# A fused attention and feed-forward kernel: the second stage's work order in tables of half steps

## The chip, the cores and the metric

The kernel runs on one core of one Trainium2 chip. The metric is device time in microseconds, from the launch to the end on that core.

## The reference

For x of 4 batches x 1024 rows x 512 columns (f32) the program computes, with xn the normalised rows:

```
xn = layernorm(x)
q, k, v = xn Wq^T, xn Wk^T, xn Wv^T          # 16 heads of 32, 4 batches: 64 (batch, head) pairs
p = softmax(causal(q k^T / sqrt(32)))         # 1024 x 1024 for each head
a = (p v) Wo^T
g = silu((xn Gate) * gate_scale);  u = (xn Up) * up_scale      # 512 -> 1536, weights rounded to fp8 values
f = ((g * u) Down) * down_scale               # 1536 -> 512
out = x + a + f
```

## The kernel before, in words

The first stage (`prepare`, about the first 285 us) normalises x, forms q, k and v and writes them to DRAM. The second stage (`attend`) is the one that is changed. It loops over 16 iterations (`NIT`), and each iteration over 4 heads (`s` = 0 to 3), so head n = 4 it + s of 64. A head's work is cut into steps `u`, and k counts the steps of the whole iteration. Every engine has its own program, written by walking the same steps and asking tables what is to be done at each; the engines then meet through semaphores. Nothing reorders the work afterwards: each engine, and the SP queue that issues the DMAs, takes its instructions strictly in the written order.

Numbers are kept as two fp16 parts, high and low, hence many operations come in pairs. The names used below:

- PE: `scores` of unit 0 to 5 (called E0 to E5 here; L1457), `scores_of_row` for the last two blocks of rows (R0, R1; L1471, L1475), `maxima_scores` of unit 0 to 7 for head n+2 (M0 to M7; L210), `values` of row block i for head n-1 (PV0 to PV7; L1495), `turn_maxima` (TURN; L263), gate and up products of feed-forward part f (G0 to G11 and U0 to U11; L1519), `down` of half i and piece j (DN(i,j); L1533), and `project` (PJ; L1541). Down works on the tile of the iteration before; project runs only from iteration 4 on (`LAG`).
- ACT: the exponential of unit u (exp0 to exp5, L1273), its high part (L1263), the exponential of a row block (L1280) and its high part (L1287), `tanh_of_gate` (L1294), `high_of_fuse` (L1302), `high_maxima` (L247, written as m_part), and the high part of the attention rows (L1330).
- DVE: maxima (L233, L238, L1399), low parts, `swiglu`, `normalise`, `copy_row` (L270), `scale_down` and `add_output` (L1371).
- POOL: causal selection, low parts (L1064, L1216, L1198, L1194), `low_maxima`.

What ties them where the change touches them: R1 overwrites a pair of banks that unit 2's exponential must have read; M0 overwrites the bank of the first row block, so it waits for that block's exponential; G0 needs the tile of xn that SP loads (`load_tile`, L1088), and SP may only issue this load when U11 of the last tile has been done; PV7 needs the second row block of the head before, turned by a DMA (`turn_row`, L1100) that SP issues behind that load. TURN's result is copied by DVE into a row, which SP stores into the next head's q (`store_row`, L200); E0 of the next head waits for it. DN(1,0) needs the copy made of the TURN before it, since both use the bank `misc`. `start_values` makes PE wait for the low parts of all units.

```
pe.wait_ge(exp_done, NE * n + 3)                     # R1
pe.wait_ge(row_exp, 2 * n + 1)                       # M0
pe.wait_ge(xt_loaded, 16 * (it + 1))                 # G0
pe.wait_ge(row_turned[ROWS.index(i)], 16 * (n + 1))  # PV6, PV7
```

Of the kernel before, what the change touches and what calls it, by code (L numbers as in the profile page):

```python
# [47 lines left out]
HEADS_PER_IT = 4  # L48
# [58 lines left out]
U = 9  # L107
# [29 lines left out]
DOWN_STEP = {0: [(0, 0), (0, 1)], 1: [(0, 2)], 2: [(0, 3)], 3: [(0, 4)], 4: [(0, 5)],
             9: [(1, 0), (1, 1)], 10: [(1, 2)], 11: [(1, 3)], 12: [(1, 4)], 13: [(1, 5)]}  # L140
# [24 lines left out]
def of_head(table, n, u):


    found = [(table[u], n)] if u in table else []
    if u + U in table and n > 0:
        found.append((table[u + U], n - 1))  # L170
    return found
# [884 lines left out]

# [642 lines left out]
```

## Time and profile before

| | |
|---|---|
| median of 3 timed runs | 1288.54 us |
| lowest, highest | 1285.94, 1290.28 us |
| span of the profiled execution | 1287.4 us |
| first matmul of the second stage | 287.67 us |
| PE busy | 1230.8 us, 96% |
| DVE, ACT, POOL busy | 80%, 70%, 68% |

No time of its own is listed for the profiled execution beside its span, which runs from the first instruction to the last. Matmuls overlap one another in the array, so the duration of one (276 ns for 256 columns) is longer than the distance to the next; the distances between starts tell how fast PE goes.

### The profile page before, as it was taken

What the parts mean: (1) busy time and instruction counts of PE and PEld (TensorE: products, weight loads), DVE (VectorE), ACT (ScalarE), POOL (GpSimd) and SP (SyncE); (2) the same over time, 40 slices, a digit from 0 to 9 for tenths busy, and PEclk for the clock granted to TensorE, in tenths of its full rate; (3) what the DMA queues carried; (4) which work ended last, traced back from release to release, by engine and by line L of the source; (5) the groups of instructions that cost most, each with busy time, mean ns of one, the idle gap of its engine ahead of it and who ended that gap; (6) DMA issues with size and microseconds to landing.
All of it is one profiled execution on the core that took longest, in us unless ns stands there. A gap on an engine that the chain in (4) does not pass through costs nothing.

```text
span 1287.4 us, 32439 instructions
## 1 busy us (share of the span) xinstructions
PE 1230.8 (96%) x11756; PEld 822.8 (64%) x11756; DVE 1036.1 (80%) x2615; ACT 895.2 (70%) x1527; POOL 873.5 (68%) x1017
## 2 busy tenths in 40 slices
PE   4999999997999999999999999999999999999988
PEld 3444444445766767676777677777767677777663
DVE  8888887877877888788878788888888888878762
ACT  4322323228878888788888788888878888888770
POOL 1333232107877787788888888978878788888882
PEclk9999999998999999999999999999999999999999
DMA  8599998855645475666667676767686766767655
GB/s 271 161 250 243 256 258 232 203 152 120 135 96 129 96 151 99 145 114 148 127 138 153 127 153 125 157 104 166 115 158 114 160 121 137 143 128 165 105 113 121
DMA packets 427599, 196.07 MB, mean 152 GB/s; under 512 B 339248, under 2 KB 396592, under 8 KB 427440
## 3 DMA queue, kind: packets, MB, share of 16 engines
q1 hardware_dynamic: 409024, 177.22, 63.2%
q10 hardware_dynamic: 18416, 16.78, 4.9%
q8 instruction: 94, 1.54, 0.5%
q14 instruction: 65, 0.53, 0.1%
HBM read 72.89 MB, written 42.21 MB: 89 GB/s over the span
## 4 chain that ended last, share of the span: by engine, by line
PE 40%; POOL 16%; ACT 8%; issue 6%; DVE 5%; DMA 2%; SPq 0%; ACTq 0%; POOLq 0%; DVEq 0%
PE bank L1519 12%; PE bank L1533 12%; POOL row L1216 7%; PE bank L1495 6%; PE pair L210 3%; PE pair L1457 3%; POOL fuse L1198 3%; POOL probs L1064 3%; ACT probs L1263 3%; PE pair L1471 2%; POOL p L1210 2%; DMA p_t<-row 2%; ACT row L1287 2%; PE pair L1541 2%; DVE row_top L1399 2%
## 5 line engine op out<-in xcount | busy, mean ns | idle before, releaser
L1273 ACT ACTIVATE p<-pair,s_exp 128x512 f32<-128x512 f32 (+1 forms) x384 | 243.4, 634 | 143.3 <-PE pair L1457 142.0
L1216 POOL TENSOR_TENSOR row<-row 128x896 f16<-128x896 f32 (+1 forms) x128 | 256.2, 2011 | 7.7 <-ACT row L1287 7.7
L1263 ACT CAST probs<-p 128x512 f16<-128x512 f32 (+1 forms) x384 | 214.9, 560 | 15.1 <-POOL p L1210 12.6
L1064 POOL TENSOR_TENSOR probs<-p,probs 128x512 f16<-128x512 f32 x192 | 221.1, 1155 | 0.2
L1519 PE MATMUL bank<-shared,wu 128*128 128x256 f16 x1536 | 202.7, 276 | 0.0
L1519 PE MATMUL bank<-shared,wg 128*128 128x256 f16 x1536 | 202.5, 275 | 0.0
L1533 PE MATMUL bank<-wd,fuse 128*128 128x512 f16 x768 | 191.7, 380 | 0.8 <-DVE ff_out L1380 0.8
L1399 DVE TENSOR_REDUCE row_top<-pair 128x1 f32<-128x896 f32 (+1 forms) x128 | 147.5, 1152 | 35.4 <-PE pair L1475 34.9
L1210 POOL TENSOR_SCALAR_AFFINE_SELECT p<-p 128x128 f32<-128x128 f32 (+1 forms) x256 | 109.6, 433 | 93.2 <-ACT p L1273 91.3
L1198 POOL TENSOR_TENSOR fuse<-fu,fuse 128x512 f16<-128x512 f32 x96 | 118.5, 1235 | 65.3 <-ACT fuse L1302 65.1
L1519 PEld LDWEIGHTS bank<-shared,wg 128*128 128x128 f16 x1536 | 143.2, 98 | 25.0 <-DMA shared<-xn_parts 0.8
L1519 PEld LDWEIGHTS bank<-shared,wu 128*128 128x128 f16 x1536 | 144.1, 99 | 22.3 <-issue 0.2
L1280 ACT ACTIVATE row<-pair,row_bias,s_exp 128x896 f32<-128x896 f32 (+1 forms) x128 | 148.3, 1158 | 0.3 <-DVE row_bias L1402 0.3
L233 DVE CUSTOM_DVE_ANT_0 junk<-pair,mask 128x128 bf16<-128x128 f32 x252 | 116.8, 482 | 34.9 <-PE pair L210 34.2
L1457 PE MATMUL pair<-q_st,k_st 98*128 98x256 f16 (+3 forms) x640 | 136.5, 278 | 1.2 <-PEq L285 1.0
L1495 PE MATMUL bank<-v_sb,probs 128*128 128x65 f16 x2688 | 134.3, 193 | 2.6 <-DVE attn L1362 2.6
L1495 PEld LDWEIGHTS bank<-v_sb,probs 128*128 128x128 f16 x2688 | 120.0, 97 | 25.2 <-issue 3.0
L210 PE MATMUL pair<-k_st,q_st 96*128 96x128 f16 x504 | 125.5, 309 | 7.6 <-issue 6.9
L1287 ACT CAST row<-row 128x896 f16<-128x896 f32 (+1 forms) x128 | 126.7, 990 | 0.0
L1387 DVE SCALAR_TENSOR_TENSOR ga<-th,bank 128x256 f32<-128x256 f32 x192 | 79.7, 415 | 43.8 <-ACT th L1294 43.6
L1064 DVE TENSOR_TENSOR probs<-p,probs 128x512 f16<-128x512 f32 (+1 forms) x192 | 112.1, 597 | 2.1 <-ACT probs L1263 2.1
L1533 PEld LDWEIGHTS bank<-wd,fuse 128*128 128x128 f16 x768 | 68.6, 97 | 61.1 <-issue 1.4
(155 smaller groups left out, 2106.0 us busy)
## 6 DMA issues: line engine op xcount, KB each, us to landing
q_st<-q_parts SPq DMA_DIRECT2D x192, 64.0 KB, 2.3
k_st<-k_parts SPq DMA_DIRECT2D x192, 64.0 KB, 2.0
v_parts<-res SPq DMA_DIRECT2D x8, 1056.0 KB, 6.8
v_sb<-v_parts SPq DMA_DIRECT2D x64, 132.0 KB, 2.2
xn_parts<-x_t SPq DMA_DIRECT2D x16, 512.0 KB, 8.8
q_parts<-qk_st SPq DMA_DIRECT2D x32, 256.0 KB, 5.5
k_parts<-qk_st SPq DMA_DIRECT2D x32, 256.0 KB, 4.2
shared<-xn_parts SPq DMA_DIRECT2D x16, 512.0 KB, 4.9
```

The costliest lines, as they stand in the source:

```text
L210: nc.tensor.matmul(banks[u % len(banks)][:, 0:w], rows.q_st[i][part, blk * P:(blk + 1) * P], rows.k_st[i][part, k0:k0 + w], start=True, st ...
L1064: ops.tensor_tensor(probs[n % 2][:, LO, at], p32[e % RING][:, 0:UNIT_WIDTH[u]], probs[n % 2][:, HI, at], ALU.subtract).then_inc(signal, 1)
L1198: nc.gpsimd.tensor_tensor(fuse_pair(LO, p), fu[p % FU][:, :], fuse_pair(HI, p), ALU.subtract).then_inc(fuse_lo, 1)
L1216: nc.gpsimd.tensor_tensor(row16[r][:, w:2 * w], row32[r][:, :], row16[r][:, 0:w], ALU.subtract).then_inc(row_lo, 1)
L1263: nc.scalar.copy(probs[n % 2][:, HI, u * 512:u * 512 + w], p32[e % RING][:, 0:w]).then_inc(p_hi, 1)
L1273: nc.scalar.activation(p32[e % RING][:, 0:w], st_bank[u % 2][:, 0:w], ACT.Exp, scale=s_exp[:, :]).then_inc(exp_done, 1)
L1287: nc.scalar.copy(row16[r][:, 0:row_width(r)], row32[r][:, :]).then_inc(row_hi, 1)
L1399: nc.vector.tensor_reduce(row_top[:, r:r + 1], row_bank[r][:, 0:row_width(r)], AX.X, ALU.max).then_inc(row_red, 1)
L1457: mm = nc.tensor.matmul(st_bank[u % 2][:, at:at + w], k_st[s][:, j * P:(j + 1) * P], q_st[s][:, q0:q0 + w], start=True, stop=True)
L1495: mm = nc.tensor.matmul(o_half[:, i % (QB // 2), :], probabilities(n, i, j, part), v_sb[s][:, j, 0:VN], start=(j == 0 and part == HI), sto ...
L1519: mm = nc.tensor.matmul(ff_bank[f % 2][:, h * FT:(h + 1) * FT], (wg8, wu8)[h][:, kc, f * P:(f + 1) * P], xt[:, part, kc, :], start=(part = ...
L1533: mm = nc.tensor.matmul(misc[:, :], fuse[:, part, f, i * P:(i + 1) * P], wd8[:, f, :], start=(f == 0 and part == HI), stop=(f == FC - 1 an ...
```

## The change

The tables get 18 half steps per head where there were 9 steps, one table for each kind of operation and engine, and PE's feed-forward tables exist twice: for iterations 0 to 3 (EARLY) and for 4 to 15 (LATE). Most entries are the old ones doubled. What stands elsewhere than before (half steps of a head, or of the iteration where the table runs over four heads):

- PE: M3 from 12 to 11 (ahead of E3); PV1 from 2 to 3 (behind the down or project piece of step 2); the wait for all low parts from PV7 to PV5; DN(1,0) from the start of head 1 to the end of head 0; TURN of head 2 behind U7; in late iterations G0 from 8 to 7, G1 from 12 to 9, G10 from 62 to 61; in early iterations U0 from 10 to 8, U9 from 54 to 57, G11 from 66 to 65.
- ACT: `high_maxima` from behind exp1 and the high part of unit 0 to ahead of exp1; the high part of the attention rows one half step earlier in head 1; `high_of_fuse` of pair 0 from 30 to 28 in early iterations.
- DVE: the reduction of M5 from 14 to 13, which puts it ahead of `swiglu` 0 in head 0.
- POOL: the low part of the attention rows from 42 to 40 in head 2, and in late iterations that of fuse pair 4 from 60 to 63, behind the first row block.

```diff
-U = 9
+U = 18
...
-M_STEP = {4: (0, 1), 5: (2,), 6: (3, 4), 7: (5,), 8: (6, 7)}
-PV_STEP = {1: (0, 1), 2: (2,), 3: (3,), 5: (7,), 6: (6,), 7: (5,), 8: (4,)}
+M_STEP = {8: (0, 1), 10: (2,), 11: (3,), 12: (4,), 14: (5,), 16: (6, 7)}
+PV_STEP = {2: (0,), 3: (1,), 4: (2,), 6: (3,), 10: (7,), 12: (6,), 14: (5,), 16: (4,)}
+UNITS_FOR = {0: 3, 5: NE}
...
+def of_ffn(what, it, k):
+    found = []
+    for i, at in ((it - 1, k + STEPS), (it, k)):
+        if 0 <= i < NIT:
+            found += [(f, i) for f in (LATE_FF if i >= LAG else EARLY_FF)[what].get(at, ())]
     return found
...
                         if n > 0:
-                            if u in (1, 5):
-                                start_values(n - 1, (s + 3) % 4, it if s == 0 else it + 1, 3 if u == 1 else NE)
                             for i in PV_STEP.get(u, ()):
+                                if i == 0:
+                                    pe.wait_ge(v_loaded[(s + 3) % 4], 16 * (it if s == 0 else it + 1))
+                                if i in UNITS_FOR:
+                                    start_values(n - 1, UNITS_FOR[i])
                                 values(n - 1, (s + 3) % 4, i)
```

PE in head 3 of iteration 1 (an early one), before: the third row is G9, the fourth U9, then come E1 (two rows), R0 (three), PV0 and PV1 (x6), E2.

```order
L1519 MATMUL bank<-shared,wu 128x256 x8
L1457 MATMUL pair<-q_st,k_st 128x512
L1519 MATMUL bank<-shared,wg 128x256 x8
L1519 MATMUL bank<-shared,wu 128x256 x8
L1457 MATMUL pair<-q_st,k_st 128x384
L1457 MATMUL pair<-q_st,k_st 128x128
L1471 MATMUL pair<-k_st,q_st 128x512
L1471 MATMUL pair<-k_st,q_st 128x384
L1475 MATMUL pair<-mask_bf,ident_bf 128x128
L1495 MATMUL bank<-v_sb,probs 128x65 x6
L1457 MATMUL pair<-q_st,k_st 128x256 x2
```

The same place in the changed kernel:

```order
L1527 MATMUL bank<-shared,wu 128x256 x8
L1467 MATMUL pair<-q_st,k_st 128x512
L1527 MATMUL bank<-shared,wg 128x256 x8
L1467 MATMUL pair<-q_st,k_st 128x384
L1467 MATMUL pair<-q_st,k_st 128x128
L1481 MATMUL pair<-k_st,q_st 128x512
L1481 MATMUL pair<-k_st,q_st 128x384
L1485 MATMUL pair<-mask_bf,ident_bf 128x128
L1505 MATMUL bank<-v_sb,probs 128x65 x6
L1527 MATMUL bank<-shared,wu 128x256 x8
L1467 MATMUL pair<-q_st,k_st 128x256 x2
```

U9 moved from ahead of E1 to ahead of E2; what stands ahead of E2 is the same in all.

PE in head 0 of a late iteration, from PV3 (x8) on, before: DN(0,4), M0, M1, DN(0,5), G0, M2, PV7 (x16), U0, and at the end TURN and G1.

```order
L1495 MATMUL bank<-v_sb,probs 128x65 x8
L1533 MATMUL bank<-wd,fuse 128x512 x4
L210 MATMUL pair<-k_st,q_st 128x128
L210 MATMUL pair<-k_st,q_st 128x256
L1533 MATMUL bank<-wd,fuse 128x512 x4
L1519 MATMUL bank<-shared,wg 128x256 x8
L210 MATMUL pair<-k_st,q_st 128x384
L1495 MATMUL bank<-v_sb,p_t 128x65 x16
...
L1495 MATMUL bank<-v_sb,p_t 128x65 x14
L263 MATMUL bank<-ident,m_part 12x128
L1519 MATMUL bank<-shared,wg 128x256 x8
```

The same place in the changed kernel:

```order
L1505 MATMUL bank<-v_sb,probs 128x65 x8
L1541 MATMUL bank<-wd,fuse 128x512 x4
L1527 MATMUL bank<-shared,wg 128x256 x8
L225 MATMUL pair<-k_st,q_st 128x128
L225 MATMUL pair<-k_st,q_st 128x256
L1541 MATMUL bank<-wd,fuse 128x512 x4
L1527 MATMUL bank<-shared,wg 128x256 x8
L225 MATMUL pair<-k_st,q_st 128x384
L1505 MATMUL bank<-v_sb,p_t 128x65 x16
...
L1505 MATMUL bank<-v_sb,p_t 128x65 x14
L278 MATMUL bank<-ident,m_part 12x128
```

G0 now stands ahead of M0, and G1, which stood behind TURN, ahead of M2 and PV7.

ACT in head 3 of iteration 1, before: tanh and `high_of_fuse` of part 8 and pair 3, exp1, the high part of unit 0, `high_maxima`, tanh and exp2.

```order
L1294 ACTIVATE th<-bank,half_gs 128x256
L1302 CAST fuse<-fu 128x512
L1273 ACTIVATE p_3<-pair,s_exp 128x512
L1263 CAST probs<-p_2 128x512
L247 ACTIVATE m_part<-mx 128x6
L1294 ACTIVATE th<-bank,half_gs 128x256
L1273 ACTIVATE p_4<-pair,s_exp 128x512
```

The same place in the changed kernel:

```order
L1314 ACTIVATE th<-bank,half_gs 128x256
L1322 CAST fuse<-fu 128x512
L262 ACTIVATE m_part<-mx 128x6
L1293 ACTIVATE p_3<-pair,s_exp 128x512
L1283 CAST probs<-p_2 128x512
L1314 ACTIVATE th<-bank,half_gs 128x256
L1293 ACTIVATE p_4<-pair,s_exp 128x512
```

Only the small m_part row moved, from behind exp1 and a high part to ahead of exp1.

## Rows read from the trace of the kernel before

**Rows 1.** The page: busy time of the engines; clock granted to PE in 40 slices.

```profile
PE 1230.8 (96%) x11756; PEld 822.8 (64%) x11756; DVE 1036.1 (80%) x2615; ACT 895.2 (70%) x1527; POOL 873.5 (68%) x1017
...
PEclk9999999998999999999999999999999999999999
```

**Rows 2.** Busy times of a stretch: PE, PEld, DVE, ACT, POOL, clock, DMA share, GB/s.

```profile
600.00:700.00 100.00, 99.86 (x1084) 72.81 (x1081) 84.30 (x238) 84.96 (x151) 82.59 (x92) 1.00 0.65 133
```

**Rows 3.** PE's waits, whole span: us in total, times, longest.

```profile
PE pair L1471 <- ACT p L1273: 13.7, 11, 1.6
...
PE pair L210 <- issue: 6.9, 10, 0.9
...
PE bank L1495 <- DMA p_t<-row: 2.6, 3, 1.0
```

**Rows 4.** Timeline of PE, iteration 1, head 3 (start, us, engine, line, operation).

```profile
392.28 1.04 PE L1519 MATMUL bank<-shared,wu 128*128 128x256 f16 x8
393.15 0.38 PE L1457 MATMUL pair<-q_st,k_st 98*128 98x384 f16 x2
...
393.99 0.38 PE L1457 MATMUL pair<-q_st,k_st 98*128 98x256 f16 x2
...
395.87 0.60 PE L1471 MATMUL pair<-k_st,q_st 96*128 96x512 f16 x2 [1.31 <-ACT p L1273]
```

**Rows 5.** Timeline of ACT in the same head.

```profile
392.74 0.62 ACT L1302 CAST fuse<-fu 128x512 f16<-128x512 f32 x1
393.57 0.69 ACT L1273 ACTIVATE p<-pair,s_exp 128x512 f32<-128x512 f32 x1 [0.21 <-PE pair L1457]
...
394.67 0.21 ACT L247 ACTIVATE m_part<-mx 128x6 f16<-128x6 f32 x1
...
395.13 0.69 ACT L1273 ACTIVATE p<-pair,s_exp 128x512 f32<-128x512 f32 x1
```

**Rows 6.** Busy times of two stretches around such waits (columns as in rows 2).

```profile
379.00:385.00 6.00, 5.02 (x46) 3.62 (x47) 4.34 (x14) 5.21 (x8) 4.50 (x7) 0.72 0.33 86
440.00:446.00 6.00, 3.96 (x51) 3.13 (x51) 5.66 (x17) 6.00 (x11) 4.24 (x8) 1.00 0.53 123
```

**Rows 7.** Timeline of PE, head 0 of iterations 10 and 6: M0 and PV7.

```profile
951.17 0.33 PE L210 MATMUL pair<-k_st,q_st 96*128 96x128 f16 x2
...
954.44 0.34 PE L1495 MATMUL bank<-v_sb,p_t 128*128 128x65 f16 x6 [1.03 <-DMA p_t<-row]
...
711.46 0.33 PE L210 MATMUL pair<-k_st,q_st 96*128 96x128 f16 x2
...
714.52 0.47 PE L1495 MATMUL bank<-v_sb,p_t 128*128 128x65 f16 x10 [0.75 <-DMA p_t<-row]
```

**Rows 8.** Timeline of SP at those two places: issues of the load and the turning.

```profile
945.78 0.57 SPq L1088 DMA_DIRECT2D shared<-xn_parts  x1
946.45 3.71 SPq L1100 DMA_TRANSPOSE p_t<-row  x1
...
705.91 0.73 SPq L1088 DMA_DIRECT2D shared<-xn_parts  x1
```

**Rows 9.** From issue to landing: load 945.78, turning 946.45, load 705.91.

```profile
DMA to landing us min/median/max: 4.5/4.5/4.5
...
DMA to landing us min/median/max: 7.9/7.9/7.9
...
DMA to landing us min/median/max: 6.6/6.6/6.6
```

**Rows 10.** Timeline of PE (TURN, head 2; E0, head 3) and SP, iteration 8.

```profile
807.34 0.22 PE L263 MATMUL bank<-ident,m_part 128*12 128x128 f16 x1
...
808.64 0.65 SPq L200 DMA_DIRECT2D q_st<-m_row  x1
...
811.46 0.38 PE L1457 MATMUL pair<-q_st,k_st 98*128 98x512 f16 x1
```

**Rows 11.** DMA throughput from 808.6 to 812.0 us in 40 slices.

```profile
GB/s 0 0 0 0 0 0 0 0 0 0 0 0 0 0 0 15 21 0 0 0 0 0 0 51 166 220 217 226 208 214 220 205 208 202 184 214 157 238 389 401
```

More of the change, by code:

```diff
@@ L162, in at_step @@
+def of_ffn(what, it, k):
[3 more added lines that the diff above has]
+            found += [(f, i) for f in (LATE_FF if i >= LAG else EARLY_FF)[what].get(at, ())]
     return found
 def of_head(table, n, u):
[L168 to L171, printed above, removed]
+    found = [(what, n - 1) for what in table.get(u + U, ())] if n > 0 else []
+    return found + ([(what, n) for what in table.get(u, ())] if n < NH else [])
@@ L1055, in over_iterations, with over_steps @@
                 step(it, it >= LAG)
+        def over_steps(step):
+            for it in range(NIT):
+                for s in range(HEADS_PER_IT):
+                    for u in range(U):
+                        step(it, s, u)
+            for u in range(U):
+                step(NIT, 0, u)
         def take_low(eng, ops, units, u, n, signal):
@@ L1332, in _, with step @@
-            over_iterations(iteration)
-            take_high(NE - 1, NH - 1)
-            for k in range(STEPS, STEPS + 3):
-                for f, t in at_step(TANH_STEP, NIT - 1, k):
+            def step(it, s, u):
+                n, k = HEADS_PER_IT * it + s, s * U + u
+                for unit, head in of_head(EXP_STEP, n, u):
+                    exponentials(unit, head)
+                for unit, head in of_head(HIGH_STEP, n, u):
+                    take_high(unit, head)
+                for r, head in of_head(ROW_EXP_STEP, n, u):
+                    exponentials_of_row(r, head)
+                for r, head in of_head(ROW_HIGH_STEP, n, u):
+                    high_of_row(r, head)
+                for _, head in of_head(MAX_HIGH_STEP, n, u):
+                    if head + 1 < NH:
+                        high_maxima(nc, act, rows, head + 1, (head + 1) % 2)
+                for f, t in of_ffn("tanh", it, k):
@@ L1336, in _ @@
                     tanh_of_gate(f, t)
-                for p, t in at_step(FUSE_STEP, NIT - 1, k):
+                for p, t in of_ffn("fuse_high", it, k):
                     high_of_fuse(p, t)
+                if LAG <= it < NIT:
+                    for i in SPLIT_STEP.get(k, ()):
+                        r = it - LAG
+                        act.wait_ge(o_done, 2 * HEADS_PER_IT * it)
+                        wait(act, turned, 16 * (2 * r + i))
+                        nc.scalar.copy(a_part[:, HI, :], attention_rows(i, r)).then_inc(split_link, 1)
@@ L1608, in _ @@
                 down(0, piece, NIT - 1)
[L1609 to L1610 removed]
+            for i in (7, 6):
+                values(NH - 1, 3, i)
+            start_values(NH - 1, NE)
+            for i in (5, 4):
                 values(NH - 1, 3, i)
```

212 lines of the change are left out of this document (97 added, 115 removed).

## The prediction

> **What bounds the kernel now.** I read the page's busy times first: PE 96%, DVE 80%, ACT 70%, POOL 68% [rows 1]. Busy PE could hide gaps, since matmuls overlap, so I then cut the span into stretches. From 600 to 700 us PE is busy for 99.86 of 100 us, with the full clock, while DVE, ACT and POOL stand at 83 to 85% [rows 2]. In the timeline the starts are packed too: eight matmuls of 256 columns take 0.87 us from the first to the next group (392.28 to 393.15, rows 4), that is 109 ns each, and 256 columns at 2.4 GHz are 107 ns. So from iteration 4 on (about 540 us) the kernel is a solid block of PE work, the same work in both kernels, and reordering it can win only what PE waits there. PE's waits, summed over the whole span, name all that matters [rows 3]: 13.7 us in 11 waits of R1 (L1471) for ACT's exponential of unit 2, 6.9 us in 10 waits of M0 (L210) for the first row block's exponential, and 2.6 us in 3 waits of PV7 for the turned rows. The first two lie almost wholly in iterations 0 to 3, where heads 2 and 3 (in iteration 0 all heads) have no down and no project pieces between E2, R1 and M0. The third lies in late iterations. All of it is some 23 us, under 2% of the span, and the change touches a part of it. A difference within 0.3% (3.9 us) can't be told from none here; the three runs lie 4.3 us apart.
>
> **U9 behind R0, and high_maxima ahead of exp1 (early head 3, four times).** In head 3 of iteration 1, PE issues U9 at 392.28, E1 at 393.15, E2 at 393.99, and R1 only at 395.87, after a wait of 1.31 us [rows 4]. ACT ends the fuse cast at 393.26 (the next could start there: 392.74 + 0.62 less the 0.1 by which records overlap), but exp1 starts at 393.57, having been idle 0.21 us for E1. Then follow a high part, m_part at 394.67, tanh, and exp2 at 395.13 [rows 5]. From exp1 to exp2 are 1.56 us of ACT without a gap, of which m_part is 0.10 (394.67 to the next start at 394.77). Now E1 comes 0.87 us earlier, so ACT no longer waits for it: exp1 gains its 0.31 us (393.57 less 393.26), gives 0.10 to m_part which now stands ahead of it, and gets the 0.10 back before exp2. So exp2, R1, the row block's exponential and M0 come 0.31 us sooner. The tanh between needs U9, which now ends some 0.3 us before ACT comes to it; E2 has the same work ahead of it and keeps its place. Four heads: 4 x 0.31 = **1.2 us gained**. The bounds: nothing, if U9's delay makes tanh late by as much, and 4 x (0.31 + 0.10) = 1.6.
>
> **high_maxima elsewhere.** In early head 2 and in the heads of iteration 0, ACT has a queue ahead of exp1 already, so m_part only moves ahead of it and exp2 starts as before: 0, at most 6 x 0.10 = 0.6. In late heads R1 waits for nothing: 0.
>
> **G0 and G1 ahead of M0 and PV7 (late head 0, twelve times).** Between M0 and PV7 stood M0, M1, DN(0,5), G0, M2: 2.07 us where nothing waits. Now G0 and G1 come ahead as well, and PV7 stands 2 x 0.87 - 0.87 = 0.87 us later in the order. That gives the turned rows 0.87 us more. But G0 now stands where M0 stood, 1.04 us earlier, so the load of xn has that much less. In iteration 10 M0 is at 951.17 and PV7 at 954.44, 1.20 us late [rows 7]. The load landed at 945.78 + 4.5 = 950.28, before G0's new place; the turning landed at 946.45 + 7.9 = 954.35 [rows 8, 9], and PV7's new place is 951.17 + 2.07 + 0.87 = 954.11. So a wait of 1.20 becomes 0.3: 0.9 gained. In iteration 6 PV7 was 0.99 us late (714.52 less 711.46 and 2.07); there the load landed at 705.91 + 6.6 = 712.51 [rows 7 to 9], and G0's new place is 711.46, so G0 now waits 1.05 and PV7 no longer. That is 0.1 lost: the wait changes its name and not its size. Since both transfers sit in one queue, one behind the other, this exchange is the rule. Of the twelve, four are late at all; by the same sums the other two give a loss of 0.1 and nothing. I take **0.7 us gained**. Bounds: all of PV7's waits, 2.6 us [rows 3], gained, and, if every load landed a microsecond later than G0's new place with the turning close behind, 12 x 0.1 = 1.2 lost.
>
> **What costs nothing, and its cover.** DN(1,0) at the end of head 0 needs the copy of TURN. From TURN to the next head's E0 are 4.12 us (807.34 to 811.46), and store_row, which needs the copy, is issued 1.30 us after TURN [rows 10]. DN(1,0) now stands two feed-forward groups nearer, at 4.12 - 2 x 0.87 = 2.4 us, so 1.1 us are spare. It also makes head 1's exp0 0.87 us later, but ACT had over a microsecond of idle time ahead of exp1 there. TURN in head 2 moves behind U7, so the row has 3.25 us instead of 4.12 to reach the next E0. The store is issued at 808.64, and its few packets run in the 16th and 17th slice of 0.085 us, 1.4 us later [rows 10, 11]. TURN at 808.21 plus 0.6 for the copy, 0.2 for SP and 1.4 gives 810.4, against 811.46: a microsecond spare. M3 ahead of E3 needs only M1 reduced, G10 ahead of M0 leaves M0 there before DVE, which is still normalising, comes to it. PV1 and the wait for the low parts moved behind work that was ready. On POOL the attention part and the fuse pair change places with parts of which the rows to be turned profit by about 0.7 us, but SP is then still busy with issues ahead of the turning, so it stays there. DVE's M5 ahead of swiglu 0 delays G2's release by 0.7 us, and G2 stands more than that behind.
>
> On the row's landing a rule bears: the Trainium skill, in DMA: Bandwidth & Descriptors (Anatomy of one DMA), gives a transfer a fixed cost of about 2.0 us, most of it the receipt after the last byte. By it the row would be there at about 808.21 + 0.8 + 2.0 = 811.0 (an estimate from that page), still ahead of E0, so the sum would be the same but with 0.4 us spare, not 1.1. The trace shows no landing for this store, only its packets.
>
> **Sum.** 1.2 + 0.7 = 1.9 us. The profiled execution's span goes from 1287.4 to about 1285.5; the median of the runs is 1.1 above that span, so 1288.5 - 1.9 = **1286.6**.
>
> **The rivals.**
> *The clock goes with the waits.* The stretch 379 to 385 had a mean granted clock of 0.72, though 440 to 446, with the same kind of waits, had 1.00 [rows 6]. PE fell to 1.2 GHz for 0.28 x 6 / 0.5 = 3.4 us, which loses 1.7 us of work at 2.4 GHz. I count five such dips after waits of R1 and M0 in iterations 0 to 3, two of them in head 3. If shorter waits there keep the clock up, 2 x 1.7 = 3.4 us come on top, and five would be 8.5: 1283.2, at the extreme 1278. Against it: the wait only shrinks from 1.31 to 1.0, and equal waits end both ways. Chance 0.2.
> On this the Trainium skill, in TensorE: Matmul & The Clock Gate (Part 1), says that the gate's phase is free-running and the cold part varies from run to run. By that such dips would come and go without the change; the trace, with waits alike and dips unlike, agrees.
> *The order is covered everywhere, nothing moves.* If U9's tanh takes back what E1 gives and PV7's wait only becomes G0's, the time is 1288.5. It is on the near side of my forecast, and the measurement couldn't tell them. Chance 0.25.
> *Head 3's E0 waits for the row (slower).* If the store's receipt comes 3.25 us after TURN or later, PE waits at E0 in all 16 iterations; it decides from there on. With a landing 0.3 us past it the cost is 16 x 0.3 = 4.8 less 1.9: 1291.4. For it speaks that this is the only place where cover was taken away for all iterations at once, against it the 1.1 us above. Chance 0.1, together with the like at DN(1,0).
> The forecast as worked out has 0.45.
>
> **How the numbers follow.** Forecast and "nothing moves" both lie within 0.3% (1284.7 to 1292.4). Some of the clock rival lies faster than 1284.7, as does a small part of the forecast (several small gains of the kind that no single wait shows). The slower rival passes +3.9 us only when large. So faster 0.27, same 0.66, slower 0.07. The range runs from 1283.2, the clock rival's time, to 1289.8, which takes in "nothing moves" with the runs' own spread of over a microsecond, and leaves out the slower rival and the extreme of the clock.
>
> **What would show it.** In the changed kernel's timeline R1's wait in head 3 of iterations 0 to 3 is near 1.0 us and in head 2 still 1.4; U9 stands between R0 and E2. In late head 0 waits for the load of xn appear at G0 (L1527) where those for turned rows at PV7 shrink. PE from 600 to 700 stays at 99.8 or 99.9 us. No wait appears at E0 of head 3 or DN(1,0). The prediction is wrong if a new wait repeats in every iteration, if more or fewer dips of the clock come in iterations 0 to 3, or if iterations 4 to 15, at some 60 us each, get shorter by more than PV7's waits.

## The result and the profile after

The changed kernel takes **1277.61 us** (median of 6 runs, 1276.75 to 1279.67) against 1289.41 us (1285.94 to 1292.1, 6 runs) for the kernel before beside it: a ratio of 0.9914, 95% interval 0.99 to 0.9927, or 11.1 us less by the ratio and 11.8 by the medians. Forecast were 1286.6 us, range 1283.2 to 1289.8. The gain is far larger than the forecast's and the time lies below the range. Two runs at a much lower clock are set aside in all medians, ratios and clocks: one of act_group (2096.08 us, clock 0.569) and one of the kernel before (1311.86 us, 0.944).

The profile page of the changed kernel (busy times; clock granted to PE in 40 slices; shares of the chain that ended last), as in [rows 1]:

```profile
PE 1229.0 (96%) x11756; PEld 820.5 (64%) x11756; DVE 1048.7 (82%) x2615; ACT 891.3 (70%) x1527; POOL 871.0 (68%) x1017
...
PEclk9999999998999999999999999999999999999999
...
PE 65%; ACT 3%; POOL 3%; issue 2%; DMA 2%; DVE 1%; SPq 0%; ACTq 0%; POOLq 0%
```

Busy times look as before. The last row doesn't: the same row of the kernel before, which I had not drawn on, is

```profile
PE 40%; POOL 16%; ACT 8%; issue 6%; DVE 5%; DMA 2%; SPq 0%; ACTq 0%; POOLq 0%; DVEq 0%
```

POOL, ACT and DVE, 29% of what had set the end, are down to 7%. The stretch 600 to 700 us (columns as in [rows 2]) is now wholly PE:

```profile
600.00:700.00 100.00, 100.00 (x1115) 73.88 (x1113) 85.76 (x239) 85.94 (x152) 85.60 (x92) 1.00 0.63 135
```

PE's waits, whole span, as in [rows 3] (R1 is now L1481, M0 L225, values L1505, G0 L1527):

```profile
PE pair L1481 <- ACT p L1293: 10.3, 10, 1.4
PE pair L225 <- issue: 6.3, 10, 0.8
...
PE bank L1527 <- DMA shared<-xn_parts: 0.8, 1, 0.8
...
PE bank L1505 <- DMA p_t<-row: 0.3, 1, 0.3
```

R1's waits fall by 3.4 us, M0's by 0.6, those for turned rows by 2.3, and 0.8 come back at G0. Summed, this is 5.5 us, half of what was gained, and even that is too much: a wait that shrinks can come back elsewhere in pieces too short to be marked.

The timeline gives the rest. I measure an iteration from TURN in head 3 to TURN in the next head 3, and split the span at the TURNs of head 15 (head 3 of iteration 3) and 59 (head 3 of iteration 14). TURN prepares the next head, so the last head, 63, has none, and eleven late iterations end in a TURN of head 3:

| stretch of the profiled execution, us | before | after |
|---|---|---|
| start to first E0 | 287.67 | 286.14 |
| E0 to TURN of head 15 | 233.87 | 229.95 |
| TURN of head 15 to TURN of head 59, 11 late iterations | 659.22 | 655.13 |
| of these, one without a wait for DMA | 59.68 | 59.43 |
| rest | 106.60 | 105.69 |

**Late iterations** are each 0.25 us shorter where PE waits for no DMA: 11 x 0.25 = 2.75; the other 1.3 are the waits for the load and for turned rows. These vary from one execution to the next: the stretch takes 659.22 us here and 658.80 to 660.40 in four other executions with the same late order, while the changed kernel has 655.13 and 655.10 (the table under the experiments). Where does a solid block of PE work get 0.25 us? Before, head 3 of the iteration whose E0 is in [rows 10] ends so (timeline of PE):

```profile
820.17 0.66 PE L1495 MATMUL bank<-v_sb,p_t 128*128 128x65 f16 x16
820.95 0.22 PE L263 MATMUL bank<-ident,m_part 128*12 128x128 f16 x1
821.11 0.39 PE L1457 MATMUL pair<-q_st,k_st 98*128 98x256 f16 x2
```

and after, in one of the late iterations:

```profile
753.51 0.65 PE L1505 MATMUL bank<-v_sb,p_t 128*128 128x65 f16 x16
754.09 0.22 PE L278 MATMUL bank<-ident,m_part 128*12 128x128 f16 x1
754.24 0.39 PE L225 MATMUL pair<-k_st,q_st 96*128 96x512 f16 x1
```

From PV7's start to TURN's are 0.78 us before and 0.58 after, and it is so in all eleven (0.78 to 0.80, and 0.58 or 0.59). TURN waited 0.2 us; only 0.13 to 0.15 of it are idle time of PE, too short to be marked as a wait. The other 0.05 lie ahead of PV7 in the same head. What released it stands in the chain of the kernel before, 804 to 821 us (start, us, what; 15 of its pieces, from POOL's fuse on):

```profile
804.92 1.16 POOL fuse L1198
806.08 1.11 POOL a_part L1194
807.19 1.12 POOL probs L1064
808.31 3.93 POOL row L1216 x2
812.25 0.71 POOL p L1210
...
813.03 0.04 ACT probs L1263
...
813.24 0.48 ACT th L1294
...
813.74 0.43 DVE ga L1387
...
814.20 0.48 DVE fu L1394
814.68 1.01 DVE row_top L1399
...
817.57 1.15 DVE row_top L1399
...
819.39 0.07 DVE attn L1362
...
820.23 0.67 DVE shared L1371
820.91 0.04 issue
820.95 0.22 PE bank L263
```

Read upwards from the last row: TURN waits for `add_output` (both use `misc`), which stands behind M0's and M1's maxima, `normalise` and `row_top` on DVE; DVE was late from ACT's tanh, tanh from the high part ahead of it, and that from POOL's causal selection, which stood behind 3.93 us of rows and, before them, the low part of the attention rows (`a_part`). The two ends of the link on ACT, before and after:

```profile
813.03 0.30 ACT L1263 CAST probs<-p 128x128 f16<-128x128 f32 x1 [0.47 <-POOL p L1210]
```

```profile
745.89 0.29 ACT L1283 CAST probs<-p 128x128 f16<-128x128 f32 x1
```

**Early iterations.** In head 3, R1 waited 1.31 us [rows 4], and now:

```profile
388.37 0.38 PE L1467 MATMUL pair<-q_st,k_st 98*128 98x512 f16 x1
...
390.59 1.03 PE L1527 MATMUL bank<-shared,wu 128*128 128x256 f16 x8
391.46 0.38 PE L1467 MATMUL pair<-q_st,k_st 98*128 98x256 f16 x2
...
392.77 0.60 PE L1481 MATMUL pair<-k_st,q_st 96*128 96x512 f16 x2 [0.74 <-ACT p L1293]
```

Head 2 goes from 1.40 to 1.21. Yet an early iteration with the full clock takes 59.05 us before and 58.71 after, 0.34 less and not the 0.76 by which the two waits shrink. In head 3 R1 starts 4.40 us after E0, for 4.69 before, and not 0.57 sooner, because PV0 now starts 0.29 us later behind R0 (0.35 us after R0's last piece, for 0.06). Behind the two feed-forward parts that follow M0 and M1, M2 then comes 0.13 us later than before, and 0.06 in head 2.

**The clock.** Such an iteration with one stretch at 1.2 GHz takes 60.7 us before and 60.2 after. From E0 to TURN 15, before has five stretches at 1.2 GHz, after has three (one of double length). Over its six runs the changed kernel has a mean granted clock of 0.9947. The clocks of the six runs of the kernel before beside it are not listed; five other sets of it have means of 0.9912 to 0.9919. A run at half the clock for part of its time loses (1 - mean clock) x time: 10.4 to 11.3 us before and 6.8 after, so 3.6 to 4.5 us of the 11.

So the gain is 2.75 (late iterations) + 1.3 (waits for the load and turned rows, one execution each) + 1.4 (early, 4 x 0.34, with iteration 0 taken to be like the others) + 3.6 to 4.5 (clock), 9 to 10 us of the 11 to 12. The remaining 1 to 3 us stay open. The table's first stretch is no part of them: its order is the same in both kernels, and 1.4 of its 1.5 us are a wait of the first stage for a DMA (`x_t<-x_part`, 2.5 us before, 1.1 after). Nor are the 0.9 of its last stretch safe: a second execution of the changed kernel takes 104.58 us there, 1.1 less than this one.

### The profile page after: what moved, and what is told of

It is laid out like the page before. It is cut to its first block, busy times and chain, and to the rows that moved or that the text cites. A ratio compares the mean times of both kernels' runs of the same rounds, so it can differ in the third digit from the quotient of the medians.

```text
span 1276.9 us, 32439 instructions
## 1 busy us (share of the span) xinstructions
PE 1229.0 (96%) x11756; PEld 820.5 (64%) x11756; DVE 1048.7 (82%) x2615; ACT 891.3 (70%) x1527; POOL 871.0 (68%) x1017
## 4 chain that ended last, share of the span: by engine, by line
PE 65%; ACT 3%; POOL 3%; issue 2%; DMA 2%; DVE 1%; SPq 0%; ACTq 0%; POOLq 0%
PE bank L1527 22%; PE bank L1541 12%; PE bank L1505 10%; PE pair L225 6%; PE pair L1467 5%; PE bank L1549 4%; PE pair L1481 4%; PE pair L1549 2%; POOL row L1241 1%; ACT p L1293 1%; ACT probs L1283 1%; DMA a_t<-a_part 1%; PE bank L278 1%; DMA p_t<-row 1%; POOL probs L1089 1%
## 5 line engine op out<-in xcount | busy, mean ns | idle before, releaser
L1527 PE MATMUL bank<-shared,wg 128*128 128x256 f16 x1536 | 201.0, 274 | 1.3 <-DMA shared<-xn_parts 0.8
L1527 PE MATMUL bank<-shared,wu 128*128 128x256 f16 x1536 | 201.2, 274 | 0.0
L1541 PE MATMUL bank<-wd,fuse 128*128 128x512 f16 x768 | 194.6, 381 | 0.8 <-DVE ff_out L1393 0.8
L1527 PEld LDWEIGHTS bank<-shared,wg 128*128 128x128 f16 x1536 | 144.9, 98 | 34.4 <-DMA shared<-xn_parts 1.3
L1527 PEld LDWEIGHTS bank<-shared,wu 128*128 128x128 f16 x1536 | 143.0, 98 | 20.3
L1505 PEld LDWEIGHTS bank<-v_sb,probs 128*128 128x128 f16 x2688 | 127.0, 97 | 38.6 <-issue 3.8
L1505 PE MATMUL bank<-v_sb,probs 128*128 128x65 f16 x2688 | 142.9, 193 | 2.6 <-DVE attn L1375 2.2
L225 PE MATMUL pair<-k_st,q_st 96*128 96x128 f16 x504 | 134.8, 309 | 6.4 <-issue 6.3
L1089 DVE TENSOR_TENSOR probs<-p,probs 128x512 f16<-128x512 f32 (+1 forms) x192 | 125.7, 668 | 2.0 <-ACT probs L1283 2.0
L1223 POOL TENSOR_TENSOR fuse<-fu,fuse 128x512 f16<-128x512 f32 x96 | 111.9, 1166 | 18.8 <-ACT fuse L1322 17.7
L253 DVE TENSOR_REDUCE mx<-pair 128x1 f32<-128x512 f32 x128 | 88.0, 688 | 23.1 <-PE pair L225 21.3
```

What stands on the lines that cost most here:

```text
L225: nc.tensor.matmul(banks[u % len(banks)][:, 0:w], rows.q_st[i][part, blk * P:(blk + 1) * P], rows.k_st[i][part, k0:k0 + w], start=True, st ...
L1089: ops.tensor_tensor(probs[n % 2][:, LO, at], p32[e % RING][:, 0:UNIT_WIDTH[u]], probs[n % 2][:, HI, at], ALU.subtract).then_inc(signal, 1)
L1505: mm = nc.tensor.matmul(o_half[:, i % (QB // 2), :], probabilities(n, i, j, part), v_sb[s][:, j, 0:VN], start=(j == 0 and part == HI), sto ...
L1527: mm = nc.tensor.matmul(ff_bank[f % 2][:, h * FT:(h + 1) * FT], (wg8, wu8)[h][:, kc, f * P:(f + 1) * P], xt[:, part, kc, :], start=(part = ...
L1541: mm = nc.tensor.matmul(misc[:, :], fuse[:, part, f, i * P:(i + 1) * P], wd8[:, f, :], start=(f == 0 and part == HI), stop=(f == FC - 1 an ...
```

## The experiments

All kernels are the changed one with some tables put back: "old" means that all entries stand where they stood before. In each fence - is the kernel that the edit starts from. Ratios are to the kernel before on the same chip. The columns R1 are the waits in early heads 2 and 3; late is an iteration without a wait for DMA; 15 to 59 is the stretch of the table above; clock is the mean granted clock of the runs.

| kernel | median us | ratio, 95% interval | R1 | late | 15 to 59 | clock |
|---|---|---|---|---|---|---|
| neutral | 1288.92 | 1.0004, 0.9995 to 1.0013 | 1.39, 1.31 | 59.69 | 660.40 | 0.9918 |
| pool_split | 1285.42 | 0.9974, 0.9958 to 0.999 | 1.39, 1.31 | 59.43 | 657.45 | 0.9917 |
| after_split42 | 1282.86 | 0.9956, 0.9943 to 0.9969 | 1.21, 0.74 | 59.79 | 657.65 | 0.9935 |
| act_group | 1284.58 | 0.997, 0.9957 to 0.9983 | 1.21, 1.22 | 59.68 | 659.31 | 0.9926 |
| max_high | 1286.82 | 0.9991, 0.998 to 1.0002 | 1.39, 1.21 | 59.68 | 658.75 | 0.9926 |
| fuse28 | 1285.62 | 0.9981, 0.9969 to 0.9993 | 1.31, 1.31 | 59.69 | 659.40 | 0.9933 |
| pe_early | 1284.61 | 0.9967, 0.9955 to 0.9979 | 1.39, 0.74 | 59.69 | 658.80 | 0.994 |
| u9_only | 1285.96 | 0.9982, 0.9973 to 0.999 | 1.40, 0.74 | 59.69 | 659.75 | 0.9932 |
| pe_late | 1290.12 | 1.0015, 1.0003 to 1.0027 | 1.58, 1.31 | 59.79 | 659.09 | 0.9908 |
| no_pe_late | 1280.92 | 0.9937, 0.9925 to 0.9949 | 1.21, 0.74 | 59.42 | 656.41 | 0.9936 |
| no_pe_late2 | 1280.48 | 0.9934, 0.992 to 0.9947 | 1.21, 0.74 | 59.42 | 655.70 | 0.9936 |
| after_again | 1278.67 | 0.9924, 0.9909 to 0.9939 | 1.21, 0.74 | 59.43 | 655.10 | 0.9937 |
| pool_pe_late | 1288.62 | 1.0001, 0.9991 to 1.0011 | 1.58, 1.31 | 59.43 | 657.53 | 0.9913 |
| gates_late | 1297.64 | 1.007, 1.0055 to 1.0084 | 1.40, 1.31 | 60.56 | 668.50 | 0.9922 |
| gates_m5 | 1287.71 | 0.9996, 0.9985 to 1.0007 | 1.40, 1.31 | 59.67 | 657.82 | 0.9915 |
| pe_rest | 1291.97 | 1.0026, 1.0013 to 1.0039 | 1.58, 1.31 | 59.78 | 660.80 | 0.99 |
| fill_m0 | 1275.12 | 0.9897, 0.9882 to 0.9912 | 0.74, 0.74 | 59.43 | 654.79 | 0.997 |
| fill_r1 | 1296.16 | 1.0041, 1.0019 to 1.0063 | 0.36, 0.36 | 59.42 | 656.12 | 0.9901 |

**neutral: the new tables with every entry at its old place.** The diff is the sum of all the edits below taken back, and of one that no run tests alone: POOL's low part of fuse pair 4 in late iterations (60 to 63). It is in the changed kernel, after_split42 and the two no_pe_late, and not in pool_split; late iterations without a wait for DMA take 59.42 to 59.43 us with it (no_pe_late) and 59.43 without (pool_split), so it shows nothing there.

> The new tables filled with the old places, so every engine's order is that of the kernel before up to the last head. A control: 1.000, and heads' distances as before. If the form of the tables or the placing of the program had a share in the gain of 11 us, this would be faster.

Nothing is gained or lost. So the form of the program, its length and its loops are worth nothing, and the moves are all.

**pool_split: only POOL's low part of the attention rows (old otherwise).**

```diff
-SPLIT_LOW_STEP = {26: (0,), 42: (1,)}
+SPLIT_LOW_STEP = {26: (0,), 40: (1,)}
```

> The kernel before in half steps, with one move alone: POOL's low part of the attention rows in head 2 from half step 42 to 40. Theory A (POOL frees ACT): in late head 2 POOL no longer idles for a fuse pair, ends the two row blocks some 0.7 us sooner, ACT's wait for POOL's selection in head 3 goes (0.47 us before), and the tanh, swiglu, normalise and add_output that follow each other there come 0.3 us sooner, so TURN of head 3 no longer waits 0.3 us: 11 or 12 iterations x 0.25 to 0.3 = 2.7 to 3.4 us, about 1286.2. Theory B (PE's order did it, G10 ahead of M0): nothing here, 1289.4, and TURN still stands 0.3 us behind PV7.

**after_split42: the changed kernel with that one entry taken back.**

```diff
-SPLIT_LOW_STEP = {26: (0,), 40: (1,)}
+SPLIT_LOW_STEP = {26: (0,), 42: (1,)}
```

> The changed kernel with POOL's attention low part put back to half step 42. Theory A (POOL sets ACT, DVE and so TURN back): a late iteration without a DMA wait takes 59.7 to 59.8 us again for 59.43, 11 to 12 iterations: 3 to 4.5 us slower than the changed kernel, about 1281.5. Rival (in the full set PE's order alone holds TURN free): 1277.6.

The pair settles the late iterations. One entry on an engine that is 68% busy takes them from 59.69 to 59.43 us with the old order, and from 59.43 back to 59.79 with the new one, where TURN starts 0.83 us after PV7 and its wait is long enough to be marked:

```profile
755.01 0.22 PE L278 MATMUL bank<-ident,m_part 128*12 128x128 f16 x1 [0.18 <-DVE shared L1384]
```

11 x 0.26 = 2.9 of the 3.3 us that pool_split gained by its ratio (1.3 to 5.4 by the interval); in the stretch it is 660.40 - 657.45 = 2.95 against neutral, and less against the other executions of the old late order, which vary by 1.6. Taken back, the entry costs 4.2 to 5.3 us by the medians of the two measurements of the changed kernel. Of this, 657.65 - 655.13 = 2.5 are in the stretch (11 x 0.36 = 4.0, less 1.4, since the longer iterations leave no load late), and 0.3 to 1.5 are clock ((0.9937 or 0.9947 - 0.9935) x 1280). The last microsecond or so is not accounted for. Where the time lay on POOL, before and after:

```profile
804.92 1.16 POOL L1198 TENSOR_TENSOR fuse<-fu,fuse 128x512 f16<-128x512 f32 x1 [1.61 <-ACT fuse L1302]
```

```profile
736.54 1.16 POOL L1219 TENSOR_TENSOR a_part<-attn,a_part 128x512 f16<-128x512 f32 x1 [0.82 <-ACT a_part L1349]
```

Before, POOL stood idle for the fuse cast and had `a_part` still to do behind it; now it does `a_part` in that gap, and the rows follow 0.7 us sooner: they start 3.87 us ahead of head 3's E0 after (741.01 and 744.88) and 3.19 ahead of it before (808.27 and 811.46). ACT's high part behind the selection comes 0.56 us sooner by the same measure. The 0.7 us are those that the prediction gave the rows.

**act_group, max_high, fuse28: ACT's moves together, and two of them alone (old otherwise).**

```diff
-MAX_HIGH_STEP = {2: (0,)}
+MAX_HIGH_STEP = {1: (0,)}
-SPLIT_STEP = {24: (0,), 40: (1,)}
+SPLIT_STEP = {23: (0,), 40: (1,)}
-FUSE_HIGH_EARLY = {36: (1,), 42: (2,), 54: (3,), 60: (4,), 74: (5,), 30: (0,)}
+FUSE_HIGH_EARLY = {28: (0,), 36: (1,), 42: (2,), 54: (3,), 60: (4,), 74: (5,)}
```

> The kernel before in half steps, with ACT's moves alone: high_maxima ahead of exp1, the attention high part one half step earlier, high_of_fuse of pair 0 at 28 in early iterations. Theory A: R1's wait in head 2 of iterations 1 to 3 falls from 1.40 to about 1.21 us, because POOL gets its fuse pair and so its selection done sooner; 0.1 to 0.2 us in ten heads: 1 to 1.5 us, about 1288.2. Rival: m_part only changes places with exp1 and nothing moves, 1289.4, R1 still waits 1.40. Dips of the clock after these waits may add or take 1.7 us each.

> The kernel before in half steps, with high_maxima ahead of exp1 alone. Of the ACT group's 3.5 us the theory gives most to the fuse cast at 28 (POOL's fuse pair and selection sooner), so here: R1's wait in head 2 stays 1.40, in head 3 falls by 0.10 (1.31 to about 1.21), 4 x 0.1 us, 1288.5. Rival: high_maxima carries the group's gain, about 1285.5.

> Theory A: of the ACT group's gain only fuse pair 0 at half step 28 shortens R1's wait in early head 2, from 1.39 to about 1.2 us, through ACT and POOL's fuse pair; head 3 stays at 1.3 and late iterations at 59.7. Four heads of 0.19 are 0.8 us: 1288.0, a ratio of 0.9985 to 1. Rival: the cast only changes places with a tanh or an exponential, R1 keeps 1.39 in head 2, and the time is that of before (ratio 0.999 to 1.0015).

max_high has only the first pair, fuse28 only the third. `high_maxima` shortens R1's wait in head 3 by 0.10, and the iteration with the full clock not at all (59.07 us against 59.06 in neutral). The fuse cast takes 0.09 off R1's wait in head 2, and head 2 from TURN to TURN goes from 15.18 to 15.07; the remaining 0.1 in act_group (1.21) needs both. So neither expectation for fuse28 holds exactly: its 0.19 is the two moves' together. All three times fall by more than these tenths allow, and the clock is 0.9926 (act_group and max_high) and 0.9933 (fuse28) against 0.9918 (neutral).

**pe_early and u9_only: PE's early feed-forward pieces (old otherwise).**

```diff
-GATE_EARLY = {..., 62: (10,), 66: (11,)}
+GATE_EARLY = {..., 62: (10,), 65: (11,)}
-UP_EARLY = {10: (0,), 14: (1,), ..., 52: (8,), 54: (9,), 62: (10,), 68: (11,)}
+UP_EARLY = {8: (0,), 14: (1,), ..., 52: (8,), 57: (9,), 62: (10,), 68: (11,)}
```

> The kernel before in half steps, with PE's early tables alone (U9 behind R0, G11 and U0 earlier, iterations 0 to 3). By the prediction's step: R1 in head 3 comes 0.2 to 0.3 us sooner four times, about 1 us: 1288.4. Theory that the clock goes with these waits: two or three dips of 1.7 us vanish on top, 1284 to 1286. Rival: G11 ahead of E3 takes it back, 1289.4.

> The kernel before in half steps, with U9 behind R0 in iterations 0 to 3 alone. If U9 carries what PE's early tables gave (4.3 us): R1's wait in head 3 at 0.74 us, mean granted clock at 0.993 to 0.994 for 0.9915, 3 to 4 us gained, 1285.3. Rival: G11 ahead of E3 and U0 at 8 carry half of it, by stretching the work around the waits: 1 to 2 us gained here, 1287.

u9_only has only U9's 54 to 57. R1's wait falls from 1.31 to 0.74, but head 3 from TURN to TURN only from 13.10 to 12.95. The 0.31 forecast for it is 0.15 in the iteration. Four of these are 0.6 us in u9_only; in pe_early, an iteration with the full clock takes 59.01 us, so G11 and U0 take two thirds of it back. Yet the kernels gain 2.3 (u9_only) and 4.3 us (pe_early). The clock accounts for about 2 and 3.6 of that ((0.9932 - 0.9916) x 1286, (0.994 - 0.9912) x 1286).

**pe_late: PE's other moves, with M5's reduction on DVE (old otherwise); no_pe_late: the changed kernel without them.** Repeated with the changed kernel beside it as no_pe_late2 and after_again.

```diff
-M_STEP = {8: (0, 1), 10: (2,), 12: (3, 4), 14: (5,), 16: (6, 7)}
-MAX_STEP = {8: (0, 1), 10: (2,), 12: (3, 4), 14: (5,), 16: (6, 7)}
-PV_STEP = {2: (0, 1), 4: (2,), ...}
-UNITS_FOR = {0: 3, 7: NE}
-TURN_STEP = {12: (0,), 30: (1,), 48: (2,), 64: (3,)}
-DOWN_STEP = {..., 18: ((1, 0), (1, 1)), ...}
-GATE_LATE = {8: (0,), 12: (1,), ..., 62: (10,), 66: (11,)}
+M_STEP = {8: (0, 1), 10: (2,), 11: (3,), 12: (4,), 14: (5,), 16: (6, 7)}
+MAX_STEP = {8: (0, 1), 10: (2,), 12: (3, 4), 13: (5,), 16: (6, 7)}
+PV_STEP = {2: (0,), 3: (1,), 4: (2,), ...}
+UNITS_FOR = {0: 3, 5: NE}
+TURN_STEP = {12: (0,), 30: (1,), 49: (2,), 64: (3,)}
+DOWN_STEP = {..., 16: ((1, 0),), 18: ((1, 1),), ...}
+GATE_LATE = {7: (0,), 9: (1,), ..., 61: (10,), 66: (11,)}
```

> The kernel before in half steps, with PE's other moves alone (late G0, G1, G10; DN(1,0), TURN of head 2, M3 with M5's reduction, PV1, the wait for the low parts). Theory A: only PV7's waits shrink (3.7 us before in four iterations, 1 to 2 us left as waits of G0 or PV7), TURN of head 3 keeps its 0.3 us: 1.5 to 2.5 us gained, about 1287.4. Theory B: these moves also free TURN, 4 to 5.5 us gained, about 1284.6. By the prediction's sum 0.7 us gained, 1288.7.

> The changed kernel with PE's other moves (late G0, G1, G10, DN(1,0), TURN, M3, PV1, the wait for low parts, M5's reduction) put back. If the groups add up, it lacks what they do: alone they cost 1.9 us, so this would be 1276 to 1278, as fast as the changed kernel or faster, with PV7's waits back at 3 us and an ordinary late iteration at 59.43. If they pay only once POOL's move has freed TURN (the theory from the two traces: their extra 0.1 us per iteration vanishes, their 1.3 to 2.5 us at PV7 stay), this is 1.5 to 2.5 us slower than the changed kernel, about 1279.6.

> The changed kernel without PE's late group, again, on the same chip as the changed kernel. By the first pair of results it is 3.3 us slower than the changed kernel; if the group costs time as it did alone (+1.9) and with POOL's move (+3.2), it is as fast or faster.

> The changed kernel itself, again, beside the next three on one chip, since the groups' effects don't add up across sessions. 1277.6 us within 1 us, ratio 0.991. If it comes out at 0.993 or more, the doubt over PE's late group lies in the sessions.

By itself the group costs: late iterations are 59.79 instead of 59.69 (TURN waits longer for `add_output`), R1's wait in early head 2 is 1.58 instead of 1.39. In the changed kernel, where POOL and ACT are earlier, neither cost is there. What remains is a gain at PV7, 655.1 us against 656.4 and 655.7 in the stretch, and one in early iterations, 58.71 against 58.99 to 59.04. On one chip the two stood 1.8 us apart (1278.67, 1280.48) with intervals that overlap. after_again's own ratio, 0.9924, lies between the 0.991 and the 0.993 by which its expectation would have judged, so how much of the first pair's 3.3 us was the group's stays open.

**gates_late, gates_m5, pe_rest: that group split (old otherwise).** gates_late has only GATE_LATE's pair, gates_m5 that and MAX_STEP's, pe_rest all but GATE_LATE's.

> The kernel before in half steps, with late G0, G1 and G10 alone. By the prediction's step: PV7's waits (3.4 to 3.7 us in the traces of the old order) shrink to waits of G0 for its load of 1 to 2.5 us, 0.7 to 2 us gained, about 1287.5, and early iterations as before. Theory that G10 ahead of M0 delays DVE: TURN's distance in late iterations grows from 59.69 to 59.79.

> Theory A: the wait of 0.74 us at M7 in gates_late comes from DVE, which does swiglu 0 ahead of M5's reduction. With that reduction moved ahead of swiglu 0 (the only difference to gates_late) the wait is gone, late iterations are back to 59.6 to 59.8 us, and the time is 1287 to 1289 us, 8 to 10 less than gates_late. Rival: G1 ahead of M2 holds back M7 by the order on TensorE itself or by DN(1,0), so the wait stays and the time is 1296 or more.

> The kernel before in half steps, with the rest of PE's late group (DN(1,0), TURN, M3 and M5's reduction, PV1, the wait for low parts), which acts in early iterations too. If this is what made the group cost 1.9 us: R1's wait in early head 2 at 1.58 us for 1.40, 2 to 3 us slower, about 1291. If the cost came from the gates, 1288.5.

gates_late missed its expectation by 10 us: each late iteration is 0.87 us longer. Timelines of PE and DVE in head 0 of one:

```profile
843.66 0.28 PE L225 MATMUL pair<-k_st,q_st 96*128 96x256 f16 x1 [0.74 <-DVE mx L253]
```

```profile
842.07 0.42 DVE L1400 SCALAR_TENSOR_TENSOR ga<-th,bank 128x256 f32<-128x256 f32 x1 [0.39 <-ACT th L1314]
842.53 0.48 DVE L1407 SCALAR_TENSOR_TENSOR fu<-bank,c_ff,ga 128x256 f32<-128x256 f32 x1
842.93 0.68 DVE L253 TENSOR_REDUCE mx<-pair 128x1 f32<-128x512 f32 x1
```

With G1 gone from the end of head 0, PE comes to M7 0.87 us sooner, M7 needs M5 reduced, and DVE does `swiglu` 0 first. gates_m5 moves that one reduction ahead of `swiglu` and is 10 us faster. PE's waits from 560 to 1150 us, in gates_late and then in gates_m5:

```profile
PE pair L225 <- DVE mx L253: 7.4, 10, 0.7
PE bank L1527 <- DMA shared<-xn_parts: 1.9, 2, 1.1
```

```profile
PE bank L1527 <- DMA shared<-xn_parts: 0.6, 1, 0.6
PE bank L1505 <- DMA p_t<-row: 0.3, 1, 0.3
```

So the MAX_STEP entry, which the prediction costed at nothing, is what lets G0's and G1's places pay. The two entries together are worth 660.40 - 657.82 = 2.6 us in the stretch against neutral, 1.0 against the lowest of the old late order (658.80), and nothing that the timed runs can show.

**pool_pe_late: POOL's move and PE's group (old otherwise).** The edits are those of pool_split and pe_late.

> The kernel before in half steps, with POOL's attention low part at 40 and PE's late moves together. Alone they gave -3.3 and +1.9 us. If they only add up: -1.4, about 1287.5. By the theory (PE's late moves cost 0.1 us per iteration only while DVE, held back through ACT by POOL, is late in head 3, and save PV7's waits) they give more than the first alone: late iterations of 59.43, PV7's waits at 1 us or less, -4.5 to -6 us, about 1283.5.

A miss of everything expected. The stretch shows POOL's gain (657.53, 59.43 an iteration), and the total doesn't. In the profiled execution the first E0 stands at 291.0 us, 4.7 us later than in pool_split's, with the same instructions ahead of it: there PE waits 4.2 us for the first stage's DMA (`x_t<-x_part`; 1.1 in pool_split, 3.6 in fill_m0 and pe_rest), and the clock falls once, at 190 us, as in no other profiled execution. From E0 to the end it takes 997.0 us, pool_split 998.1. So this execution lost its time ahead of the changed stage. Whether the ten other runs (1286.42 to 1290.49 us) did so too, no run tells. Against the full gain also stand three loads of xn that were late at G0 (3.4 us) and R1's wait of 1.58 in head 2.

**fill_m0 and fill_r1: beyond the change.** M0's waits (0.64 us in early heads 2 and 3) have no PE work ahead of them. fill_m0 puts G6, G10 and, in head 1, U2 there, and U5 behind R0 in head 2, as U9 is in head 3. fill_r1 starts from it and puts U5 and U9 between E2 and R1, with their tanh and `swiglu`.

```diff
-GATE_EARLY = {..., 44: (6,), ..., 62: (10,), 65: (11,)}
-UP_EARLY = {..., 26: (2,), 30: (3,), 34: (4,), 36: (5,), ..., 57: (9,), ...}
+GATE_EARLY = {..., 43: (6,), ..., 61: (10,), 65: (11,)}
+UP_EARLY = {..., 25: (2,), 30: (3,), 34: (4,), 39: (5,), ..., 57: (9,), ...}
```

```diff
-UP_EARLY = {..., 39: (5,), ..., 57: (9,), ...}
-TANH_EARLY = {..., 38: (5,), ..., 56: (9,), ...}
-SWIGLU_EARLY = {..., 40: (5,), ..., 58: (9,), ...}
+UP_EARLY = {..., 41: (5,), ..., 59: (9,), ...}
+TANH_EARLY = {..., 41: (5,), ..., 59: (9,), ...}
+SWIGLU_EARLY = {..., 42: (5,), ..., 60: (9,), ...}
```

> The changed kernel with more of the same in iterations 0 to 3: U5 of head 2 behind R0 as U9 is, G6 and G10 ahead of M0 (where PE waits 0.64 us for the row block's exponential), U2 of head 1 ahead of M0. By the theory that PE's waits in these iterations cost their length and the low clock that follows some of them: M0's waits in heads 2 and 3 vanish (8 x 0.64 = 5.1 us recorded), R1's in head 2 falls toward 0.74 (4 x 0.3), 5 to 8 us gained on the changed kernel, 1270 to 1273. Rival: ACT sets the pace of these heads and the wait goes elsewhere (R1 of the next head, or M2 for DVE): within 2 us of the changed kernel.

> The kernel fill_m0 with U5 and U9 one more place down, behind E2 where PE waits for R1, and their tanh and swiglu behind exp2. If the fill theory holds, R1's waits in heads 2 and 3 fall below 0.5 us for 0.74 or more, 2 to 4 us more than fill_m0. Rival: tanh now stands between exp2 and the row block's exponential, so that M0 waits instead: no gain on fill_m0.

fill_m0 is the fastest kernel of all, 1275.12 us (4 runs, 1272.44 to 1276.68), 2.5 and 3.6 us below the two medians of the changed kernel, where 5 to 8 were expected. Its waits are not gone but renamed:

```profile
PE pair L1481 <- ACT p L1293: 8.4, 10, 1.4
PE pair L225 <- DVE mx L248: 8.0, 10, 1.2
...
PE pair L225 <- issue: 0.9, 1, 0.9
```

M2 now waits for DVE's maxima, and an early iteration shrinks by 0.14 us only (58.57). What pays is the clock: in the profiled execution it falls once behind the first E0 (at 294 us) and then stays up through iterations 1 to 3, and over the four runs its mean is 0.997. fill_r1 has the shortest waits at R1, 0.36, and loses: M2's wait for DVE grows from 0.83 to 2.41 us in early heads 2 and 3, which neither side of its expectation had, and in the profiled execution the clock falls twice in each of iterations 1 to 3, which take 64.4 us each.

```profile
PE pair L225 <- DVE mx L248: 20.5, 9, 2.4
...
PE pair L1481 <- ACT p L1293: 5.3, 10, 1.4
```

## Why the prediction was wrong

**What bounds the kernel.** That PE's waits "name all that matters" was the first error. From 600 to 700 us PE was busy 99.86 of 100 us, and the missing 0.14 was passed over. It is the idle time ahead of the one TURN of head 3 in that window, and it comes, as a delay of 0.2 us, in each of eleven iterations. Waits this short have no mark; the distance from TURN to TURN against the sum of its matmuls shows them. The prediction named its own sign of being wrong, that iterations 4 to 15 "get shorter by more than PV7's waits", and it came: eleven of them lost 4.1 us, and PV7's three waits were 2.6.

**The step that failed** is the sentence on POOL under "What costs nothing": the rows to be turned profit, "but SP is then still busy with issues ahead of the turning, so it stays there". POOL's earlier work was followed to one of its readers, SP, and not to the other: the causal selection behind those rows, and ACT's high part that waited 0.47 us for it. From there it goes through tanh, `swiglu`, `row_top` and `add_output` to TURN. Costed at 0, it measured 3.3 us by itself (pool_split, 2.9 of them in eleven late iterations) and 4.2 or more where everything else is moved (after_split42). The chain that ended last held all of this in the kernel before, with POOL at 16%.

**The clock rival** (chance 0.2, 3.4 us on top) came in as well: 3.6 to 4.5 us in the first measurement, (0.9937 - 0.9914) x 1285 = 3.0 in after_again. "The wait only shrinks from 1.31 to 1.0, and equal waits end both ways" holds for one wait but was used for the mean of many. Neither this nor POOL's chain would alone have left the range by much (1286.6 - 3.3 = 1283.3, with the range from 1283.2); both did. The sentence of the Trainium skill, in TensorE: Matmul & The Clock Gate (Part 1), that the cold part varies from run to run agrees with the spread within a kernel (0.993 to 0.996 after); it doesn't carry over to the means, which move with the order of work from 0.99 to 0.997.

**U9 behind R0, and high_maxima** (1.2 us forecast): right in mechanism. R1 comes 4.40 us after E0 instead of 4.69, 0.29 against the 0.31 forecast. But U9 alone gives 0.15 per iteration and `high_maxima` 0; heads 2 and 3 together give 0.34, 1.4 us in four iterations, since the fuse cast at 28 and PE's order in head 2 add theirs. What the sum took for the gain, R1 and M0 coming sooner, loses half of itself at M2. The cast at 28 has no term at all in the prediction, which left head 2 at 1.4; it came out at 1.21.

**G0 and G1** (0.7 us forecast, by exchange): 1.3 in the profiled executions, and 2.4 against neutral's. The place that was worked out first kept a wait of 0.32 at PV7, with 0.3 forecast. The one whose wait was to move to G0 has none there; one of 0.8 us at G0 stands in the last iteration instead. (Those two places lie in iterations 11 and 7, whose E0s start at 944.65 and 704.94 us, and not in 10 and 6; iteration 4 starts at 525.87, not at about 540. No sum hangs on it.) Mis-sized was the cover: "DVE's M5 ahead of swiglu 0" was costed by G2's release, and is a condition for M7, without which the gates' move loses 8.8 us (gates_late).

**The slower rival** did not come: E0 of head 3 never waits for the row, in any kernel with TURN at 49. The 2.0 us of fixed cost that the prediction took from the Trainium skill, in DMA: Bandwidth & Descriptors (Anatomy of one DMA), are stated there for DMAs issued by GpSimd (POOL), and this store is issued by SP; no run shows its landing, and no term of the sum hung on it. The rest of "what costs nothing" costs nothing only in company: alone it loses 3.4 us by the ratio (pe_rest).

## What to carry to other kernels

When every engine works in order, an operation that is moved to an earlier place on an idle-looking engine moves everything behind it, so follow each reader of that engine until the chain comes back to the bound engine or finds slack of its own; the chain that ended last shows which engines still count, whatever their busy share. In a block that is 99.9% busy, compare the period with that of the bare work: here 0.2 us without a mark in each of eleven iterations were worth as much as the three marked waits of PV7 (2.6 us). Test moves in their final company and with one entry taken back, since the same moves gained or lost according to what stood around them.

## What the hardware showed that was not expected

The mean granted clock moves with the work order, although it also varies from run to run: 0.9912 to 0.9919 for the kernel before in five sets of 14 to 29 runs, 0.9937 and 0.9947 for the changed kernel, 0.9918 for neutral, 0.994 for pe_early, 0.997 for fill_m0. One stretch at 1.2 GHz lengthens an early iteration by 1.5 to 1.7 us (60.20 and 58.71 after, 60.74 and 59.05 before), so this is worth as much as the waits themselves. And in fill_r1 one kernel has two times: three runs at 1285.3 to 1288.8 us with a clock of 0.995 to 0.996, nine at 1294.1 to 1299.7 with 0.987 to 0.989. The length of the wait at R1 (0.36 us) did not decide it; whether the longer waits at M2 (2.4 us) did was not tried.
